# The third pair of a block's scores moved between the two halves of the weighing

## What is computed

```
dots = (q @ k.T) * SCALE                      # 1024 x 1024 for each head
m    = softmax(dots)
diag = diagonal(m)
keep = abs((diag - mean(diag)) / std(diag, ddof=1)) <= 1.5
valid = keep[:, None] & keep[None, :]
attn = softmax(where(valid, dots, -1e30))     # rows without a valid entry: 0
out  = attn @ v
x    = x + concat(out) @ w_out.T + b_out
```

## Time and profile before

| | us |
|---|---|
| median of 3 runs | 1895.53 (1892.8 to 1896.35) |
| the profiled execution, its own time | 1897.05 |
| its span | 1895.6 |
| PE busy | 1777.5 (94%) |
| PE weight loads busy | 1212.1 (64%) |
| DVE busy | 1326.0 (70%) |
| ACT busy | 1148.9 (61%) |
| POOL busy | 1172.7 (62%) |

### The profile page before, as it was taken

One profiled execution on the slowest core, in us unless ns is written; L12 is line 12 of the kernel. 1 busy time (PEld: TensorE's weight loads), 2 busy tenths in 40 slices (PEclk: granted clock), 3 DMA queues, 4 the chain that ended last, 5 costly groups with the idle time before them and its releaser, 6 DMA issues. The chain is left out here.

```text
span 1895.6 us, 29863 instructions
## 1 busy us (share of the span) xinstructions
PE 1777.5 (94%) x11043; PEld 1212.1 (64%) x11043; DVE 1326.0 (70%) x2493; ACT 1148.9 (61%) x1715; POOL 1172.7 (62%) x660
## 2 busy tenths in 40 slices
PE   8998999888999897899999999999999999999888
PEld 5883444334785663577777777777677777765466
DVE  5627899996345764767777777777677767778676
ACT  6326777853435447676767676766667676753554
POOL 5541777874453551377677776776767777777354
PEclk9999999999999999999999999999999999999999
DMA  2000000000001004122221222121212121200100
GB/s 100 1 1 1 1 0 1 1 0 1 0 1 50 1 1 101 36 60 56 52 60 47 61 49 66 43 67 47 60 36 71 47 60 47 57 24 12 50 6 17
DMA packets 43665, 66.03 MB, mean 35 GB/s; under 512 B 24769, under 2 KB 26177, under 8 KB 43265
## 3 DMA queue, kind: packets, MB, share of 16 engines
q1 hardware_dynamic: 43056, 63.54, 13.0%
q10 hardware_dynamic: 432, 0.59, 0.1%
q0 software_dynamic: 32, 0.00, 0.0%
HBM read 29.05 MB, written 1.24 MB: 16 GB/s over the span
## 5 line engine op out<-in xcount | busy, mean ns | idle before, releaser
L2422 POOL TENSOR_TENSOR at_e_lo<-at_e,at_e_hi 128x1024 fp32r<-128x1024 f32 x256 | 613.0, 2394 | 308.8 <-DVE at_e_hi L2397 301.8
L2179 ACT ACTIVATE at_e<-at_ps,at_dropped 128x1024 f32<-128x1024 f32 x256 | 285.7, 1116 | 216.2 <-PE at_ps L1892 200.4
L2276 DVE CUSTOM_DVE_ANT_0 at_ps<-at_ps,at_mask 128x1024 f32<-128x1024 f32 x256 | 313.4, 1224 | 5.9 <-PE at_ps L2012 5.9
L2171 ACT ACTIVATE at_ps<-at_ps,at_neg_diag 128x1024 f32<-128x1024 f32 x256 | 278.5, 1088 | 42.2 <-DVE at_neg_diag L2267 41.9
L2397 DVE CAST at_e_hi<-at_e 128x1024 fp32r<-128x1024 f32 x256 | 228.5, 892 | 23.5 <-ACT at_e L2179 20.0
L1971 PE MATMUL at_ps<-at_kq,at_qk 64*128 64x512 f32 x768 | 222.0, 397 | 13.0 <-DMA at_kq<-at_qk 5.2
L2021 PE MATMUL at_ps<-at_qk,at_kq 64*128 64x512 f32 x768 | 225.1, 399 | 1.6 <-DVE at_row_max L2276 1.1
L1892 PE MATMUL at_pv_ps<-at_e_hi,at_v_hi 64*128 64x512 f32 x980 | 225.7, 453 | 0.3 <-issue 0.3
L2022 PE MATMUL at_ps<-at_kq,at_qk 64*128 64x512 f32 x768 | 225.0, 399 | 0.0
L1972 PE MATMUL at_ps<-at_qk,at_kq 64*128 64x512 f32 x768 | 222.2, 397 | 0.0
L1056 POOL TENSOR_TENSOR mb_work<-mb_work,mb_c 128x1024 f32<-128x1024 f32 x64 | 151.8, 2372 | 96.8 <-DVE mb_work L1025 96.7
(11 more groups left out here) (392 smaller groups left out, 4149.9 us busy)
## 6 DMA issues: line engine op xcount, KB each, us to landing
at_kq<-at_qk SPq DMA_DIRECT2D x128, 256.0 KB, 4.3
at_mask<-at_mask_dram SPq DMA_DIRECT2D x32, 256.0 KB, 3.6
at_recips<-at_recip_row SPq DMA_DIRECT2D x31, 256.0 KB, 4.4
ffn_h_raw<-in_h SPq DMA_DIRECT2D x2, 1024.0 KB, 7.3
at_head_w_raw<-in_w_qkv SPq DMA_DIRECT2D x32, 64.0 KB, 3.9
x<-in_x SPq DMA_DIRECT2D x4, 256.0 KB, 4.8
moe_gate_in<-in_gate_in SPq DMA_DIRECT2D x2, 512.0 KB, 3.9
moe_up_in<-in_up_in SPq DMA_DIRECT2D x2, 512.0 KB, 4.5
```

The costliest lines, as they stand in the source:

```text
L2171: act.eng.activation(ps[:], ps[:], ACT.Exp, scale=SCALE, bias=m.small["neg_diag"][s][:, blk:blk + 1], accum_out=m.small["sums"][s][:, blk: ...
L2179: act.eng.activation(m.e[e % 2][:], slot("turned_scores", h, blk)[:], ACT.Exp, scale=SCALE, bias=m.small["dropped"][h % SLOTS][:, blk:blk ...
L2276: dve.eng.tensor_tensor_reduce(out=ps[:], in0=ps[:], in1=m.mask[h % 2][:], scale=1.0, scalar=-BIG, op0=ALU.add, op1=ALU.max, accum_out=m.s ...
L2422: pool.eng.tensor_tensor(m.e_lo[e % 3][:], m.e[e % 2][:], m.e_hi[e % 3][:].bitcast(F32), ALU.subtract).then_inc(sem["at_lo"])
```

## The change

The third pair of `scores` (high by low) is issued after the first half of `weigh` and ahead of `best`. That holds where all three stages are under way and the weighed block isn't a head's last (`t % 8` is not 7); elsewhere all three pairs stay together. `weigh` waits for e_lo at its start, and no longer for e_hi there. On DVE the small reads `negate_mean`, `negate_square`, `mask_rows` and `shift_rows` go ahead of `diagonal`; `first_stats` and `keeps` stay behind it.

```diff
-    def scores(h, blk):
+    def scores(h, blk, terms):
...
-        pe.wait_ge(sem[f"parts_move{h % 2}"], 16 * PARTS * (h // 2 + 1))
-        slot_free(pe, c, m, "scores", h, blk)
-        for n, (q, k) in enumerate(((HI, HI), (LO, HI), (HI, LO))):
+        if 0 in terms:
+            pe.wait_ge(sem[f"parts_move{h % 2}"], 16 * PARTS * (h // 2 + 1))
+            slot_free(pe, c, m, "scores", h, blk)
+        for n in terms:
+            q, k = ((HI, HI), (LO, HI), (HI, LO))[n]
...
-        mm.then_inc(sem["at_scores"])
+        if 2 in terms:
+            mm.then_inc(sem["at_scores"])
...
-        pe.wait_ge(sem["at_hi"], e + 1)
+        pe.wait_ge(sem["at_lo"], e + 1)
...
-        pe.wait_ge(sem["at_lo"], e + 1)
         mm = both_rows(banks, with_ones, [lo[:, half] for half in HALF], False, blk == BLK - 1 and turned, turned)
...
+        scored = due(t, AT_SCORES, BLK)
+        split = bool(apart and scored and weighed[1] != BLK - 1)
...
-        if at := due(t, AT_SCORES, BLK):
-            scores(*at)
+        if scored:
+            scores(*scored, (0, 1) if split else (0, 1, 2))
...
         if apart:
             weigh(*weighed, False)
+        if split:
+            scores(*scored, (2,))
         if tested:
             best(*tested)
...
+        if at := due(t, AT_MEAN):
+            negate_mean(at[0])
+        if at := due(t, AT_SQUARE):
+            negate_square(at[0])
+        if at := due(t, AT_MASK):
+            mask_rows(at[0])
+        if at := due(t, AT_SHIFT):
+            shift_rows(at[0])
         if at := due(t, AT_SCORES, BLK):
             diagonal(*at)
         if at := due(t, AT_STATS):
             first_stats(at[0])
-        if at := due(t, AT_MEAN):
-            negate_mean(at[0])
         if at := due(t, AT_SQUARE):
-            negate_square(at[0])
             keeps(at[0])
-        if at := due(t, AT_MASK):
-            mask_rows(at[0])
-        if at := due(t, AT_SHIFT):
-            shift_rows(at[0])
```

## The result

The changed kernel takes 1942.82 us, median of 4 runs (1940.1 to 1947.04), beside 1894.76 for the kernel before (4 runs on the same chip, 1892.8 to 1896.35): a ratio of 1.0242, 95% interval 1.0226 to 1.0258. The forecast was 1940.5. The profiled execution took 1945.32 (span 1943.9), 48.3 more than that of before.

A forecast was written before the change was run, and what follows sets the result against it. TensorE bounds the kernel, but chains through VectorE and ScalarE return late: 21 heads x 1.73 plus 8 x 1.08 give 45 us on 1897.05, so 1942.1 profiled; the median, 1.5 lower, is forecast at 1940.5, range 1914 to 1956.

The forecast's parts named there:

- (a): Third score pair moved behind the first half: everything released by the scores comes 0.69 later, against 0.66 to spare.
- m3: Small product of the mask in step 3 (mN is step N's): loads 1.47 later, waiting for step 2's best scores' read.
- m2: Small product of step 2: loads 0.71 later, set by ScalarE's squared deviations rather than by the best scores' read.
- (b): Two pairs between the weighing's halves: the second half's stall goes, -0.11 in a step without other work there.
- the row sums' loop: Plain step bound by scores, diagonal, sums, scores: 3.27 us against 3.31 before, taking back the stall's gain.
- (c): Small product and first half on TensorE load 0.23 earlier, though what frees the small product's slot comes later.
- (d): VectorE's small reads ahead of the diagonal: removes 0.22 wait at shift rows and 0.17 between step 2's diagonal and cast.
- (e): Weighing's wait for e_lo comes two pairs (0.46) earlier: 2 us of cover, so it costs nothing.
- The bubble alone: Rival, chance 0.04: slots are free in time and only the 0.11 stalls are saved, -15 us, 1881.
- the even exchange: Rival, chance 0.03: small products don't bind beyond today's wait; plain step goes 3.31 to 3.27, total 1895.
- m3's chain alone: Rival, chance 0.13: only step 3's small product's chain stretches, the two earlier ones lose some 0.1 between them; 1915.
- The lock: Rival, chance 0.12: one VectorE cast per head also meets GpSimd, 0.52 each, 15 us on top, 1956.

The follow-up runs named there:

- the late reciprocal: Kernel before with VectorE's new order and the two small denominator operations moved behind step 2's cast and row test: 1910.49 us, ratio 1.0072.

## Why the prediction was right

**The sum.** 45 forecast in the stretch, 46.4 measured, and the head that was computed came out within 0.14 at all seven places, within 0.10 at six of them. The sign was decided where the prediction put it: scores read by others were moved 0.69 back against 0.66 of room or none.

**(a) and the chain to m3.** Shown by three runs. Splitting step 2 alone moves m3 by 0.62; a third pair 0.46 late costs 21 us less of the stretch than one 0.69 late; and a shorter test gives back 28 us (31 of the stretch). m3's load is 4.57 behind m2 for a forecast 4.61. The 2.76 from step 4's third pair to the end of its test's read uses 0.22 from diagonal to cast, which no row of the prediction shows; it measured 2.77.

**(b)** held: the stall is gone and a plain step is unchanged within 0.05 (3.31 and 3.36 in this head), because the row sums' loop took its place with 0.21 of wait. The loop was forecast at 3.27 and came out at 3.36, which with the 0.06 by which step 4 was late puts step 5's start 0.14 behind the forecast. From there to m5 it was 0.07 less than forecast and from m5 to step 6 another 0.06, so that step 6 comes out within 0.01: that closeness is luck. That the 0.11 per step is real is shown by the turned pair in the place of the score pair, which keeps it in step 4 (3.33 to 3.22).

**(c)** had no run of its own; the added pair that it leaves behind the m's is seen in step 3 of the split in steps 3 and 6.

**(d)** was right in its place and only there. For the 0.17 between diagonal and cast 0.19 was measured (1.26 in the changed kernel, 1.45 before) and the wait at the shift rows went. What the prediction didn't say is that the same edit alone gives nothing, because m2's read then holds the diagonal back, and that it keeps the split from costing some 70 us more.

**(e)** nothing, as forecast.

**Mis-sized, and luck.** m2 is 0.10 later than forecast. ScalarE's squares end 2.38 behind the diagonal (1249.43 - 1247.05) for 2.37, as assumed; but step 1's third pair is 0.77 behind m1, not 0.70, and the diagonal 0.71 behind that (1247.05 - 1246.34), not 0.66. The heads with a projection of the values lose 1.25 and not 1.08: 8 x 0.17 = 1.4 us. The warm-up, left out, has 2.0. Against that the median stands 2.5 under the profiled execution, where 1.5 was assumed. These cancel in part, by luck, and 2.3 us remain of a difference that the profiled execution alone has at 3.2.

**The rivals.** The bubble alone and the even exchange needed room that step 4's sums and m3 don't have. m3's chain alone fell with m1 and m2, which are 0.32 and 0.81 later, not 0.1. The lock adds nothing in steps 0 to 5 of the changed kernel: the cast that met GpSimd at 1.21 us comes later now and takes 0.69, while e_lo ended before it began:

```profile
1252.82 2.37 POOL L2429 TENSOR_TENSOR at_e_lo<-at_e,at_e_hi 128x1024 fp32r<-128x1024 f32 x1 [1.62 <-DVE at_e_hi L2404]
...
1255.67 0.69 DVE L2404 CAST at_e_hi<-at_e 128x1024 fp32r<-128x1024 f32 x1
```

No cast of steps 0 to 5 takes more than 0.70 there in any of the 29 heads. In steps 6 and 7, where GpSimd also normalises, the casts are longer than before, 1.66 and 1.31 in the mean for 1.15 and 0.89; but these steps grew by only 0.02 and 0.04. That the lock was near is shown by the late reciprocal, which fell into it and lost 14 us where a gain was expected.

## What to carry to other kernels

When a stall of the busiest engine is to be filled, ask who waits for the work that fills it. Follow each chain that starts at the moved instruction through the other engines back to this one, and compare its room with the move: here 0.69 against 0.66 and less, and the loss is what remains, added up along the chain. Work with a late consumer (the turned scores) fills the same gap and keeps most of the gain, 8 of 12 us here. An edit that is neutral alone can be what another one needs, so parts are to be measured alone and together; and a small operation is priced by where it stands in an in-order queue and by what runs beside it, not by its duration alone (0.16 us here, which cost 14).

## What the runs showed of the hardware

A `tensor_scalar` on 128x8 elements, 0.16 us by itself, took 1.45 us beside GpSimd's 128x1024 operation and ended 0.03 us after it. The Trainium skill ("SBUF — State Buffer", Who interferes with whom) says that `tensor_scalar` can enter a 2-port mode and that the later of the two is then blocked for the whole instruction. By that rule the trace agrees, and it shows that an operation of 8 elements per partition pays it too, and that the wait is booked in the record as duration and not as idle time. The reciprocal and the 8x128 cast from PSUM behind it, at 0.20 and 0.27, ran when GpSimd was done, so this run doesn't tell what they would do beside it.

The traces also give the size of the wait. The cast of the earlier trace rows begins 0.67 before GpSimd's e_lo ends and takes 0.52 longer than its 0.69. With the new VectorE order alone the same cast begins 0.45 before that end (1232.09 and 1232.54) and takes 1.00, 0.31 longer. The `tensor_scalar` above began 1.42 before the end and took 1.29 longer. Each wait is the overlap less 0.13 to 0.15. Casts that begin less than 0.1 before the end, as in step 3 of the run with the shorter test (0.07), aren't longer.
